# The sum of two pairs of states: an addition of the vector engine, or a transfer that adds to its destination

## What is computed

```
dA  = exp(dt * A);  dBx = dt * B * xs
h   = scan over the tokens of  h = dA * h + dBx
y   = sum over the 16 states of  h * C,   + D * xs
y   = y * silu(z);  out = y @ W_out
```

## Time and profile before

| | |
|---|---|
| median of 3 runs | 8892.51 us (8873.36 to 8898.86) |
| profiled execution, its time | 8887.31 us |
| its span | 8885.5 us |
| busy: PE, DVE, ACT, POOL | 79%, 79%, 70%, 9% of the span |
| DMA, mean over the 16 engines | 116 GB/s |
| chain that ended last | 1% DMA, the rest of it in the last norm |

### The profile page before, as it was taken

How to read it: one execution, slowest core, us unless ns; L and a number is a source line. 1 busy time by engine, 2 the same in 40 slices (tenths; PEclk the granted TensorE clock), 3 DMA queues, 4 the chain that set the end, 5 groups by cost and what they waited for, 6 DMA issues and landing times. The chain is left out here.

```text
span 8885.5 us, 117469 instructions
## 1 busy us (share of the span) xinstructions
PE 7020.2 (79%) x33290; PEld 3894.5 (44%) x33290; DVE 7053.6 (79%) x9195; ACT 6179.2 (70%) x13424; POOL 806.7 (9%) x554
## 2 busy tenths in 40 slices
PE   6777777788888888888888888888888888888561
PEld 3444444444444444444444444444444444444330
DVE  2788888888888888888888888888888888888743
ACT  4766666677777777777777777777777777777434
POOL 0133333400000000000000000000000000000055
PEclk8988989899999999999999999999999999999775
DMA  2233333233333323333333333333333333332356
GB/s 91 105 119 119 109 109 108 92 118 117 115 120 117 118 107 123 114 119 114 115 117 115 114 115 121 113 112 115 121 117 109 122 115 117 111 122 109 127 116 199
DMA packets 282498, 1034.03 MB, mean 116 GB/s; under 512 B 37570, under 2 KB 129526, under 8 KB 273824
## 3 DMA queue, kind: packets, MB, share of 16 engines
q1 hardware_dynamic: 248352, 1009.77, 31.6%
q0 software_dynamic: 33792, 21.18, 1.5%
HBM read 951.57 MB, written 90.94 MB: 117 GB/s over the span
## 5 line engine op out<-in xcount | busy, mean ns | idle before, releaser
L1047 PE MATMUL psS<-KM,Q 128*99 128x394 f32 x4096 | 1718.4, 536 | 351.2 <-ACT PTs L578 260.8
L843 DVE TENSOR_TENSOR_SCAN hs<-dA,hs 128x1576 f32<-128x1576 f32 x512 | 1762.3, 3442 | 63.0
L572 ACT ACTIVATE P<-psS,least_s 99x197 f32<-99x197 f32 x4096 | 1413.4, 431 | 469.4 <-DVE least_s L768 466.3
L1054 PE MATMUL psS<-cst,P 99*99 99x99 f32 x8192 | 1047.9, 268 | 345.1 <-ACT P L572 300.6
L1054 PEld LDWEIGHTS psS<-cst,P 99*99 99x99 f32 x8192 | 912.2, 176 | 895.9 <-ACT P L572 654.5
L768 DVE TENSOR_REDUCE least_s<-psS 99x2 f32<-99x394 f32 x2048 | 1087.7, 562 | 261.7 <-PE psS L1047 229.6
L649 ACT ACTIVATE dA<-dt_,aneg 128x394 f32<-128x394 f32 x2048 | 1184.4, 621 | 28.9 <-DVE hs L843 18.9
L578 ACT ACTIVATE PTs<-psS 99x396 f32<-99x396 f32 x2048 | 985.9, 517 | 223.6 <-PE psS L1054 219.0
L1047 PEld LDWEIGHTS psS<-KM,Q 128*99 128x99 f32 x4096 | 626.4, 174 | 1086.9 <-ACT PTs L578 578.0
L829 DVE TENSOR_TENSOR hs<-hs,u 128x1576 f32<-128x1576 f32 x512 | 917.6, 1792 | 42.2 <-DMA hs<-bc_scratch 40.7
L1139 PE MATMUL psY<-hs,cst 128*128 128x394 f32 x2048 | 831.4, 536 | 116.1 <-DVE hs L852 115.7
(11 more groups left out here) (214 smaller groups left out, 9499.9 us busy)
## 6 DMA issues: line engine op xcount, KB each, us to landing
hs<-bc_scratch SPq DMA_DIRECT2D x512, 788.0 KB
cr<-bc_scratch SPq DMA_DIRECT2D x512, 788.0 KB
pat<-patches SPq DMA_DIRECT2D x64, 1176.0 KB, 5.9
more_scratch<-zeros SPq DMA_DIRECT2D x64, 197.0 KB, 5.2
rows_scratch<-hs SPq DMA_DIRECT2D x1, 12352.0 KB, 43.1
PTs<-more_scratch SPq DMA_DIRECT2D x24, 512.0 KB
sum_scratch<-HW SPq DMA_DIRECT2D x64, 148.5 KB
hs<-rows_scratch SPq DMA_DIRECT2D x24, 386.0 KB
```

The lines of the kernel that those rows point to most:

```text
L572: last = nc.scalar.activation(P[:, r, b, m, 0:T], psS[0:CT, 2 * r + b, m * T:(m + 1) * T], ACT.Exp, bias=least_s[:, r, b, m:m + 1], scale= ...
L843: nc.vector.tensor_tensor_scan(h, a, h, 0.0, ALU.mult, ALU.add).then_inc(scan_ready, 1)
L1047: mm(psS[0:CT, 2 * r + b, 0:2 * T].rearrange("p (e t) -> p e t", e=2), Q[:, r, b, q * CT:(q + 1) * CT], KM[:, r, h % 2 * 2:h % 2 * 2 + 2, ...
L1054: last = nc.tensor.transpose(psS[0:CT, 2 * r + b, at:at + CT], P[:, r, b, m, k * CT:(k + 1) * CT], c("ident")[0:CT, 0:CT])
```

## The change

The addition of `half` leaves DVE. In its place POOL waits for the same count of `mul_done` and queues a transfer from `hs[:, g, 2:4]` to `hs[:, g, 0:2]` (128 rows of 3152 bytes) that adds to its destination. The transfer counts up one of three semaphores `half_summed`, one for each buffer of the ring, by 16 when it has landed, and PE's `sum` waits on that one. Two semaphores that only mark a passed wait are joined with POOL's. All else stays as it was.

```diff
+        half_summed = [sem(f"half_summed{n}") for n in range(HBUF)]
+        q_waited = act_waited = pool_waited
...
+            def half(i, g):
+                pool.wait_ge(mul_done, i * MULS + MUL_OUT[g])
+                pool.sem_inc(pool_waited, 1)
+                nc.gpsimd.dma_start(hs[:, g % HBUF, 0:2, :], hs[:, g % HBUF, 2:4, :], accum_op=ALU.add).then_inc(half_summed[g % HBUF], 16)
+
...
-            loop(pool, "dve", {}, {"keep": keep, "route": route_unit})
+            loop(pool, "dve", {}, {"keep": keep, "half": half, "route": route_unit})
...
-            def half(i, g):
-                dve.wait_ge(mul_done, i * MULS + MUL_OUT[g])
-                nc.vector.tensor_tensor(hs[:, g % HBUF, 0:2, :], hs[:, g % HBUF, 0:2, :], hs[:, g % HBUF, 2:4, :], ALU.add).then_inc(half_summed, 1)
...
-                  "half": half, "ys": ys, "merge": merge, "route": route_unit})
+                  "ys": ys, "merge": merge, "route": route_unit})
...
-                pe.wait_ge(half_summed, i * QUARTERS + g + 1)
+                pe.wait_ge(half_summed[g % HBUF], ring(i, g, HBUF))
```

More of the change, by code:

```diff
@@ L242, in vit_mamba_moe @@
         names = ("open_ready loaded patches_loaded pool_ready unused_ready rows_zeroed rows_stored more_zeroed hw_ready "
-                 "q_waited ht_ready conv_done sent_all pair_free all_added fin_ready mul_done half_summed "
+                 "ht_ready conv_done sent_all pair_free all_added fin_ready mul_done "
                  "slot_ready pool_waited sent_a sent_b slots_free e_out added_a added_b ids_ready sum_ready act_setup consts_ready act_back xz_done xc_ready "
@@ L246, in vit_mamba_moe @@
                  "sp_ready scan_ready da_ready mv_ready rstd_ready act_route ht_done h2_ready lg_done gl_ready gm_ready "
-                 "score_ready act_waited xt_done e13_done fin_mv fin_ln fin_rs dve_setup weights_ready h_ready dve_back "
+                 "score_ready xt_done e13_done fin_mv fin_ln fin_rs dve_setup weights_ready h_ready dve_back "
                  "xs_ready dtm_ready dve_waited acc_done zeroed y_done ys_ready m_done dve_route sel_ready pos_done flag_set "
@@ L251, in vit_mamba_moe @@
         (open_ready, loaded, patches_loaded, pool_ready, unused_ready, rows_zeroed, rows_stored, more_zeroed,
-         hw_ready, q_waited, ht_ready, conv_done, sent_all, pair_free, all_added, fin_ready,
-         mul_done, half_summed, slot_ready, pool_waited, sent_a, sent_b, slots_free, e_out, added_a, added_b, ids_ready, sum_ready, act_setup,
+         hw_ready, ht_ready, conv_done, sent_all, pair_free, all_added, fin_ready,
+         mul_done, slot_ready, pool_waited, sent_a, sent_b, slots_free, e_out, added_a, added_b, ids_ready, sum_ready, act_setup,
          consts_ready, act_back, xz_done, xc_ready, sge_ready, sg1_ready, sgr_ready, bc_done, dtbc_ready,
          bc_stored, dtp_done, dt_ready, abs_ready, spe_ready, sp_ready, scan_ready, da_ready, mv_ready, rstd_ready,
-         act_route, ht_done, h2_ready, lg_done, gl_ready, gm_ready, score_ready, act_waited, xt_done, e13_done,
+         act_route, ht_done, h2_ready, lg_done, gl_ready, gm_ready, score_ready, xt_done, e13_done,
          fin_mv, fin_ln, fin_rs, dve_setup, weights_ready, h_ready, dve_back, xs_ready, dtm_ready, dve_waited,
```

## The result

The changed kernel takes 9727.77 us (median of 4 runs, 9727.1 to 9729.34) against 8884.59 (4 runs, 8873.36 to 8898.86): a ratio of 1.0953, 95% interval 1.0933 to 1.0972. The forecast was 9450, its range 9160 to 9950. The direction and the largest term held; 278 us more than the forecast were lost, and the rest of this text is about where.

What follows compares the result with a forecast made beforehand. The prediction took no engine to be full: DVE, PE and ACT wait in turn, paced by PE's strictly ordered list. 8887.3 + 456 (open steps) + 109 (closed steps) made 9452 us, forecast 9450, range 9160 to 9950.

Steps and rivals of the forecast that it cites:

- Part 3: Open steps: group 0's transfer queues behind the route's 32 scatters on POOL, 45.6 us a step, ten times, 456 us.
- the 1.7 of the closed steps' parts: Closed steps: DVE's gain of 3.0 us against PE's waits of 3.5 and 1.2, net +1.7 us a step, 109 us.
- The price of one transfer: From the end of output on DVE to landing: 5.3 us, say 5.4 with the wait, range 3.8 to 7.
- Groups 0, 2, 4 and 5: Closed steps: windows of 11 us and more between output and sum, so no wait of PE was counted.
- Group 6: Closed steps: 6.3 us between output on DVE and sum on PE, so the transfer just makes it.
- Part 2, the transfer of group 7: Closed steps: transfer lands at 4115.8 against PE's sum at 4113.29, a wait of 2.5 us, of which 1.2 counts.
- the prediction's own sign: Closed steps under 121 or over 133 us would show the price of a transfer to be wrong; 125 to 129 expected.
- rival 1: Slow adding transfer of 10 us or more; groups 1, 3, 6 and 7 miss, time near 10370; 12% chance.
- Part 1: DVE gives up eight additions, 7.7 us a step; 3.0 us of it counted as gain, bounds 0 and 5.
- Rival 3: DVE's time comes home whole in groups 4 to 7 and 0 to 2, 492 us against 456, 8850; 3% chance.
- Part 2, group 3: Closed steps: the transfer lands late for PE's sum in the feed-forward chain, next matmul 3.5 us later.
- window: Time from the end of a group's output on DVE, where POOL may issue, to the start of its sum on PE.

Runs made afterwards that it cites:

- all_noscatter: The changed kernel with only 2 of the 32 scatters of each route left on POOL: 9287.12 us, ratio 1.0466 to the kernel before.
- s3: The kernel before with only group 3's addition done by the transfer, the others by DVE: 9092.67 us, ratio 1.0236 to the kernel before.
- s5: The kernel before with only group 5's addition done by the transfer, the others by DVE: ratio 1.0054 to the kernel before.
- s7: The kernel before with only group 7's addition done by the transfer, the others by DVE: 9313.77 against 8883.08 us, ratio 1.0484.
- all_short0: The changed kernel with group 0's loads of hs and cr cut to one state of four from the second step on: 9468.1 us, ratio 1.0664 to before.
- all_copy: The changed kernel with a plain copy of the same bytes in place of the adding transfer: 9372.94 us, ratio 1.0557 to the kernel before.
- nohalf: The kernel before without any of the additions on DVE and with no transfer in their place: 8826.72 against 8877.04 us, ratio 0.9948.
- s4: The kernel before with only group 4's addition done by the transfer, the others by DVE: 8877.58 against 8881.11 us, ratio 1.0001.

## Why the prediction held, and where it was off

Held:

- *Part 3*, the main term. Expected 456 us for ten open steps, 45.6 each, to which the 1.7 of the closed steps' parts come. The open step grew by 49.2; all_noscatter puts the share of the scatters at 45.3 a step, 441 us in all. The parts of it: scatters 47.8 us (forecast 49.0), landing 2.0 (2), sum 0 late by 43.8 of waiting (46.9 before the deductions).
- The price of one transfer, on the average and in part by luck. I had 5.3 us from the end of `output`, for a transfer with little beside it. Such a one lands 4.2 us after the start of its issue in the median of s3, 4.6 in that of s5: the issue was put at 1.6 us, that of the scatter that adds, and takes 0.86. The median of the changed kernel, with the transfers that have company in it, is 5.7. The data term was put at 2.5 us, between the load's 1.6 and the scatter's 4.0; it is 2.28. The Trainium skill's fit ("DMA: Bandwidth & Descriptors", the anatomy of one DMA), an estimate of 2.9 us for these bytes, is met by the plain copy (2.6 at the least, 3.1 in the median) and not by the adding one: here the measurement decides.
- Groups 0, 2, 4 and 5 do not make PE wait in the closed steps read, as said, nor does group 1. Group 6, which was to be just in time, is 0.35 us late.

Off:

- *Part 2, the transfer of group 7*. This is the step that failed by most, and with it the closed step left its bounds: 133.2 us, where the prediction's own sign was that over 133 the price of a transfer is wrong. So it was, for a transfer that has company. It read "+1.5 (two loads leave at the same moment)", a wait of 2.5 us of which 1.2 would count. The row of SP's queue that it rested on is right; the size is not. Beside two loads the landing is 9.1 us in the median of s7, 4.5 over that of s5; PE waits 7.1 us, and the loss is 6.7 us a step (431 over 64), 5.5 more than forecast, 64 x 5.5 = 350 us. Two things add up: the transfer shares with 1.6 MB of loads (all_short0), and adding takes twice the engine time of a copy (all_copy). PE's idle 1.33 us covered little, since DVE's YS and norm stand behind the sum in one chain, and the way from the sum to `merge`, which begins at the lower clock, is 1.6 us longer. This is rival 1's "the loads crowd it", at one group of the four that it named. The rows for a better price were there: one load of 807 KB takes 3.7 us from its issue by the earlier trace rows, and two of them on the same engines speak for more than 1.5.
- *Part 1*. "I take 3.0 us" of 7.7. nohalf gives 50 us, 0.8 a step over all and 0.2 in a closed one, even with nothing put in DVE's place, and s4 gives none. DVE waits in turn with PE and ACT, and what it gives up shows as longer waits elsewhere. Rival 3 counted on all 492; the ceiling is a tenth.
- *Part 2, group 3*. Forecast 3.5 us a step; PE waits 2.0 to 2.1, and s3 shows a closed step no longer than before. The chain it stands in must have slack of that size; where the slack lies no run shows.
- *Left out*: group 5. Its window was wide, so I counted nothing. By itself its transfer costs 0.8 us a step by making a load late, though nothing of it shows beside group 7's. A window tells who waits for the transfer, and not whom the transfer makes wait.

The sums: forecast 456 + 64 x 1.7; found 492 for the ten open steps, of which 453 are the scatters', and 6.9 a closed step, which group 7 makes by itself. Term by term a closed step was put at -3.0 (DVE's gain), +3.5 (group 3) and +1.2 (group 7), and it is about -0.2, 0 and +6.9. That the first two errors nearly cancel is luck. What is left is group 7's error, about 5.7 a closed step, which the range had room for without having named it.

## What to carry to other kernels

Before an operation is moved from a compute engine to a DMA queue, look at three lists and not at one: what stands ahead of it in the queue of the engine that issues it (here 32 scatters, 45 us in each of ten steps), what transfers leave at the same moment (here two loads of 807 KB that leave in the 0.8 us ahead of it), and which later load it will make late. And ask for the ceiling first, by leaving the operation out altogether: one run would have said that 492 us of DVE were worth 50.

## What the runs showed of the hardware

- An adding transfer within the on-chip memory (128 rows of 3152 bytes) takes 2.28 us of each of the 16 DMA engines and comes in 144 packets, a plain copy of the same bytes 1.05 in 80; POOL needs 0.86 us to issue the first and 0.54 the second.
- With little beside it it lands 4.0 to 4.6 us after the start of its issue (s3, s5); beside 1.6 MB of loads after 9.1 (s7), beside a load of `cr` and one of the patches after 9.3 (s4), up to 10.0 in the changed kernel.
- A scatter that POOL issues while DVE's scan runs takes 3.41 us in place of 0.99, as in the earlier trace rows. The new transfer showed no such thing in the main: 0.86 us in the median, 1.3 at most.
- After a wait of 7.14 us, and of 4.01 in all_short0, PE's granted clock is 0.50 (1.2 GHz), and its next four matmuls take 2.99 us; after one of 2.04 us it is 1.00 (2.4 GHz) and they take 1.59. So a stall can be dearer than its length.
